# A graph network on one core: the opening written anew, and the turned tiles' move

## The reference

```
x = x + L0(relu(norm(x)))   # relu(mean over incoming edges @ W_l.T + b + x @ W_r.T)
x = x + L1(relu(norm(x)))   # two such convolutions with untransposed weights (L1A, L1B)
x = x + L2(relu(norm(x)))   # the means by src, residual, a layer norm with gamma and beta
x = x + L3(relu(norm(x)))   # two convolutions scaled by degrees, with self loops (L3A, L3B)
```

## Time and profile before

| | us |
|---|---|
| median of 3 runs (lowest to highest) | 646.88 (646.28 to 648.64) |
| the profiled execution | 647.0 |
| its span (first to last instruction) | 645.1 |
| PE busy | 626.6, 97% of the span |
| DVE, ACT, POOL busy | 401.5, 303.8, 85.2 |

### The profile page before, as it was taken

The page is one execution under the profiler, slowest core; times in us unless marked ns, Lnnn a source line. Parts: engine busy times, 40 slices in busy tenths (PEclk is TensorE's granted clock), DMA queues, the critical chain, the costliest instruction groups (busy, mean ns, idle before and its releaser), DMA issues.

```text
span 645.1 us, 11113 instructions
## 1 busy us (share of the span) xinstructions
PE 626.6 (97%) x3047; PEld 511.2 (79%) x3048; DVE 401.5 (62%) x875; ACT 303.8 (47%) x628; POOL 85.2 (13%) x135
## 2 busy tenths in 40 slices
PE   5989999999989999999999999999999999999997
PEld 4547767777868888888888888888888998899886
DVE  6998999977867434533434888754999730531222
ACT  4887886644423454431224342225478752565210
POOL 4442433200000000000000000000354070000000
PEclk9999999999999999999999999999999999999999
DMA  6300005457684422587550465431200000000102
GB/s 215 117 1 2 1 23 80 63 125 150 105 172 109 109 33 72 142 207 173 122 91 6 130 142 148 98 65 49 81 1 1 1 2 1 2 0 1 49 17 97
DMA packets 151843, 48.39 MB, mean 75 GB/s; under 512 B 133500, under 2 KB 137396, under 8 KB 151800
## 3 DMA queue, kind: packets, MB, share of 16 engines
q1 hardware_dynamic: 150520, 45.34, 30.8%
q10 hardware_dynamic: 1280, 2.56, 1.2%
HBM read 30.44 MB, written 17.44 MB: 74 GB/s over the span
## 4 chain that ended last, share of the span: by engine, by line
PE 86%; DVE 4%; DMA 3%; issue 2%; SPq 2%; ACT 1%; DVEq 1%; ACTq 0%
PE ps L1721 33%; PE ps L1814 23%; PE ps L1851 13%; PE ps L1877 8%; PE ps L1700 8%; DMA count_rows<-count_squares 2%; SPq L491 1%; DVE src_hot L1212 1%; DMA wstage<-in_L_gnn_W_l 1%; PE ps L1714 1%; DVE stats L1184 1%; DVE p_lo L1504 0%; ACT cstage L844 0%; DMA zT<-rows 0%; DVE own L1436 0%
## 5 line engine op out<-in xcount | busy, mean ns | idle before, releaser
L1814 PE MATMUL ps<-p_hi,cstage 128*128 128x512 f32 x400 | 156.0, 390 | 2.8 <-ACT cstage L844 2.8
L1814 PE MATMUL ps<-p_lo,cstage 128*128 128x512 f32 x400 | 155.7, 389 | 0.0
L1721 PE MATMUL ps<-w_hi,hT_hi 128*128 128x512 f32 x320 | 126.3, 395 | 0.6 <-issue 0.4
L1721 PE MATMUL ps<-w_hi,hT_lo 128*128 128x512 f32 x320 | 124.7, 390 | 0.0
L1721 PE MATMUL ps<-w_lo,hT_hi 128*128 128x512 f32 x320 | 124.6, 389 | 0.0
L1814 PEld LDWEIGHTS ps<-p_hi,cstage 128*128 128x128 f32 x400 | 75.1, 188 | 19.7 <-ACT cstage L844 2.9
L1814 PEld LDWEIGHTS ps<-p_lo,cstage 128*128 128x128 f32 x400 | 75.1, 188 | 15.5
L1212 DVE TENSOR_SCALAR src_hot<-iota,nodeT 128x640 bf16<-128x640 f16 x210 | 69.0, 384 | 5.8 <-PE ps L1700 3.7
L1700 PE MATMUL ps<-src_hot,dst_hot 128*128 128x320 bf16 x420 | 65.7, 305 | 5.8 <-DVE src_hot L1212 2.9
L1721 PEld LDWEIGHTS ps<-w_hi,hT_hi 128*128 128x128 f32 x320 | 60.1, 188 | 13.3 <-issue 0.9
L1721 PEld LDWEIGHTS ps<-w_hi,hT_lo 128*128 128x128 f32 x320 | 60.1, 188 | 12.7
(11 more groups left out here) (156 smaller groups left out, 941.3 us busy)
## 6 DMA issues: line engine op xcount, KB each, us to landing
rows<-squares SPq DMA_DIRECT2D x38, 256.0 KB, 2.5
zT<-rows SPq DMA_DIRECT2D x120, 64.0 KB, 2.5
count_rows<-count_squares SPq DMA_DIRECT2D x10, 320.0 KB, 2.2
countT<-count_rows SPq DMA_DIRECT2D x40, 80.0 KB, 3.2
x<-in_x ACTq DMA_DIRECT2D x1, 2304.0 KB
out_x<-x SPq DMA_DIRECT2D x9, 256.0 KB
wstage<-rows SPq DMA_DIRECT2D x32, 64.0 KB, 2.5
wstage<-in_L_gnn_W SPq DMA_DIRECT2D x2, 1024.0 KB, 5.7
```

Of the source, the lines that this page charges most:

```text
L1721: last = nc.tensor.matmul(ps[:, bank, :], a[:, r, k, :], w[:, slot, k, :], start=n == 0, stop=n == len(pairs) - 1)
L1814: last = nc.tensor.matmul(ps[:, AGG + r, :], cstage[:, part, k, :], p_[:, k, :], start=n == 1, stop=n == 2 * len(parts) * NT)
```

## The change

It has four parts. (1) The ranges of the windows are found without turning `reach`: each partition (an edge tile) says for all 20 windows whether it meets them (`begun`, `meets`), and an fp16 matmul of `meets` with a diagonal of tile numbers (`diag_ud`, made by POOL) puts the numbers of the meeting tiles on the window's partition; DVE then takes two maxima and derives `span` in fewer steps, and writes `tiles_of` of window 0 itself. (2) The keys are made by ACT (a copy with +1, a Sign, a copy, a scaled Sign) and POOL (a product and a sum) in fp16, and turned by fp16 matmuls with `ident16`. (3) Loads move: `src` is loaded by ACT's queue ahead of its table load; SP issues both halves of the first weight, the second weight and `x` one behind the other without waits; the first weight goes to `w_first` (in the space of `p_hi`). The turns and splits of the weights are dealt out differently around the first windows, POOL makes 2 of 20 windows of `tab` first and 18 after its keys, and `mv_now` with its copy is gone. (4) In L0, `first_tile` and DVE's `lo` of the next layer's tiles move from i = 5 and 6 to 6 and 7 (L1A and L1B keep theirs).

```diff
...
-    FIRST_W = (wstage, w_own)
+    FIRST_W = (w_first, w_own)
...
+    def load_edges(engine, k, dram, loaded):
+        engine.dma_start(e_int[:, k, 0, :], dram[0:P * P].rearrange("(t e) -> t e", e=P)).then_inc(loaded, 16)
+        engine.wait_ge(pads_set, 1)
+        engine.dma_start(e_int[0:FULL - P, k, 1, :],
+                         dram[P * P:FULL * P].rearrange("(t e) -> t e", e=P)).then_inc(loaded, 16)
+        if REST:
+            engine.dma_start(e_int[FULL - P:FULL - P + 1, k, 1, 0:REST],
+                             dram[FULL * P:E].rearrange("(t e) -> t e", t=1)).then_inc(loaded, 16)
...
+            load_edges(sp, 0, dst_dram, dst_loaded)
...
-            order = [("f", 0), ("f", 1), ("f", 2), ("v", rows[0]), ("v", rows[1])]
+            order = [("f", 0), ("f", 1), ("f", 2), ("x", None), ("v", rows[0]), ("v", rows[1])]
...
-                        sp.wait_ge(first_loaded[1], 16)
-                        sp.wait_ge(table_pe, 3)
-                        sp.wait_ge(table_step, steps_of_table)
...
+            nc.gpsimd.iota(tile_ud[:, 0, :], [[1, ETP]], base=1, channel_multiplier=0, **ramp).then_inc(ramps0, 1)
+            nc.gpsimd.iota(tile_ud[:, 1, :], [[-1, ETP]], base=ET, channel_multiplier=0, **ramp).then_inc(ramps0, 1)
+            nc.gpsimd.iota(block_lo[:, :], [[WIN, NW]], base=0, channel_multiplier=0, **ramp)
+            nc.gpsimd.iota(block_hi[:, :], [[WIN, NW]], base=WIN, channel_multiplier=0, **ramp)
+            nc.gpsimd.iota(fours[:, :], [[RING, ETP // RING]], base=ET, channel_multiplier=0, **ramp).then_inc(ramps0, 1)
             pool.wait_ge(ident0, 1)
             nc.gpsimd.affine_select(out=ident[:, :], in_=ident[:, :], compare_op=ALU.not_equal, fill=1.0,
-                                    base=0, pattern=[[-1, P]], channel_multiplier=1).then_inc(pool_consts, 1)
-            nc.gpsimd.iota(iota[:, :], [[1, NS]], base=0, channel_multiplier=0,
-                           allow_small_or_imprecise_dtypes=True).then_inc(pool_consts, 1)
-            for q, sign in ((0, 1), (1, -1)):
-                nc.gpsimd.iota(tab[:, :, q * WIN:(q + 1) * WIN], [[sign * WIN, NW], [sign, WIN]], base=sign,
-                               channel_multiplier=0, allow_small_or_imprecise_dtypes=True).then_inc(pool_consts, 1)
+                                    base=0, pattern=[[-1, P]], channel_multiplier=1).then_inc(ident0, 1)
+            pool.wait_ge(ramps0, 3)
+            nc.gpsimd.memset(fours[:, 0:1], -float(ETP))
+            for a, b in ((0, P), (P, ETP)):
+                nc.gpsimd.affine_select(out=diag_ud[:, :, a:b], in_=tile_ud[:, :, a:b], compare_op=ALU.is_equal, fill=0.0,
+                                        base=0, pattern=[[0, 2], [-1, b - a]], channel_multiplier=1).then_inc(diag_set, 1)
+            pool.wait_ge(ident0, 2)
+            nc.gpsimd.tensor_copy(ident16[:, :], ident[:, :]).then_inc(ident0, 1)
+            nc.gpsimd.iota(iota[:, :], [[1, NS]], base=0, channel_multiplier=0, **ramp).then_inc(tab_begun, 1)
+            def tab_of(a, b, done):
+                for q, way in ((0, 1), (1, -1)):
+                    nc.gpsimd.iota(tab[:, a:b, q * WIN:(q + 1) * WIN], [[way * WIN, b - a], [way, WIN]],
+                                   base=way * (1 + a * WIN), channel_multiplier=0, **ramp).then_inc(done, 1)
+            tab_of(0, 2, tab_begun)
...
+            pool.wait_ge(node_parts, 2)
+            nc.gpsimd.tensor_tensor(turned16[:, 0, :, :], e_f[:, 0, :, :], sign[:, :, :], ALU.mult).then_inc(keys_made, 1)
+            pool.wait_ge(node_parts, 4)
+            nc.gpsimd.tensor_tensor(turned16[:, 1, :, :], e_f[:, 1, :, :], shift[:, :, :], ALU.add).then_inc(keys_made, 1)
+            tab_of(2, NW, tab_full)
...
+            load_edges(act, 1, src_dram, src_loaded)
             act.wait_ge(dve_consts, 1)
             nc.scalar.activation(inner[:, 0, 3:4], eps[:, :], ACT.Sqrt)
-            for k, loaded in enumerate((dst_loaded, src_loaded)):
-                act.wait_ge(loaded, 16 * (2 + bool(REST)))
-                nc.scalar.copy(e_f[:, k, :, :], e_int[:, k, :, :]).then_inc(cast_done, 1)
-            act.wait_ge(first_loaded[1], 16)
-            act.wait_ge(x_pad_set, 1)
-            dma_rows(act, x_dram, x, x_loaded)
+            act.wait_ge(dst_loaded, 16 * (2 + bool(REST)))
+            nc.scalar.activation(e_f[:, 0, :, :], e_int[:, 0, :, :], ACT.Copy, bias=1.0).then_inc(node_parts, 1)
+            act.wait_ge(src_loaded, 16 * (2 + bool(REST)))
+            nc.scalar.activation(sign[:, :, :], e_int[:, 1, :, :], ACT.Sign, scale=-1.0, bias=middle[:, 0:1]
+                                 ).then_inc(node_parts, 1)
+            nc.scalar.copy(e_f[:, 1, :, :], e_int[:, 1, :, :]).then_inc(node_parts, 1)
+            act.wait_ge(node_parts, 2)
+            nc.scalar.activation(shift[:, :, :], sign[:, :, :], ACT.Copy, scale=NS / 2, bias=-NS / 2).then_inc(node_parts, 1)
...
-            split_first(0, range(0, 2))
-            act.wait_ge(table_step, steps_of_table)
-            act.wait_ge(pool_consts, 4)
+            act.wait_ge(table_step, FIRST_OF_TABLE)
+            act.wait_ge(tab_begun, 3)
...
             receivers(0, 0, visits_of(act, visited, 0, 0))
+            split_first(0, range(0, 2))
+            act.wait_ge(table_step, STEPS_OF_TABLE)
+            receivers(0, 1, visits_of(act, visited, 0, 1))
             split_first(0, range(2, KF))
-            receivers(0, 1, visits_of(act, visited, 0, 1))
             counts_of(0, 0)
+            act.wait_ge(tab_full, 2)
...
-                        if i == 5 + late // 2:
+                        if i == 5 + (s != L1A):
                             first_tile(0)
-                        if i == 6 + late // 2:
+                        if i == 6 + (s != L1A):
...
+            dve.wait_ge(ramps0, 3)
+            for g in range(2):
+                last = nc.vector.tensor_scalar(begun[:, g, :], block_lo[:, :], reach[:, g:g + 1], None, ALU.is_le)
+            step(last)
+            for g in range(2):
+                last = nc.vector.scalar_tensor_tensor(meets[:, g, :], block_hi[:, :], reach[:, 2 + g:3 + g],
+                                                      begun[:, g, :], ALU.is_gt, ALU.mult)
+            step(last)
             dve.wait_ge(table_pe, 1)
-            for k, tiles in enumerate((tile_up, tile_dn)):
-                last = nc.vector.scalar_tensor_tensor(marks[0:NW, k, :], ps[0:NW, TABLE, 0:ETP], block_lo[0:NW, 0:1],
-                                                      tiles[0:NW, :], ALU.is_ge, ALU.mult)
-            step(last)
-            for k in range(2):
-                last = nc.vector.scalar_tensor_tensor(marks[0:NW, k, :], ps[0:NW, TABLE, 256:256 + ETP],
-                                                      block_hi[0:NW, 0:1], marks[0:NW, k, :], ALU.is_lt, ALU.mult)
-            step(last)
-            step(nc.vector.tensor_reduce(ends[0:NW, :], marks[0:NW, :, :], AX_X, ALU.max))
-            step(nc.vector.tensor_scalar(low[0:NW, :], ends[0:NW, 1:2], 1.0, -1.0, ALU.max, ALU.mult))
-            step(nc.vector.scalar_tensor_tensor(length[0:NW, :], ends[0:NW, 0:1], -float(ET), low[0:NW, :],
-                                                ALU.add, ALU.subtract))
-            nc.vector.tensor_scalar(base[0:NW, :], low[0:NW, :], float(ET), None, ALU.add)
-            step(nc.vector.tensor_scalar(over[0:NW, :], fours[0:NW, :], length[0:NW, 0:1], None, ALU.is_lt))
+            step(nc.vector.tensor_reduce(ends[0:NW, :], ps[0:NW, TABLE, 0:2 * ETP].rearrange("p (k t) -> p k t", k=2),
+                                         AX_X, ALU.max))
+            dve.wait_ge(diag_set, 2)
+            nc.vector.tensor_scalar(base[0:NW, :], ends[0:NW, 1:2], -1.0, float(ET), ALU.mult, ALU.add)
+            step(nc.vector.tensor_scalar(over[0:NW, :], fours[0:NW, :], ends[0:NW, 0:1], ends[0:NW, 1:2],
+                                         ALU.subtract, ALU.is_lt))
             step(nc.vector.tensor_reduce(groups[0:NW, :], over[0:NW, :], AX_X, ALU.add))
-            step(nc.vector.scalar_tensor_tensor(span[0:NW, :], groups[0:NW, :], 256.0 * RING, base[0:NW, :],
-                                                ALU.mult, ALU.add))
-            dve.wait_ge(table_pe, 3)
-            step(nc.vector.tensor_copy(tiles_of[0:1, :], ps[0:1, TABLE, 0:NW]))
+            for to in (tiles_of[0:1, 0:1], span[0:NW, :]):
+                n = to.shape[0]
+                step(nc.vector.scalar_tensor_tensor(to, groups[0:n, :], 256.0 * RING, base[0:n, :], ALU.mult, ALU.add))
...
-                nc.vector.bn_aggr(mv_now[:, :], stats[:, :]).then_inc(aggr_done, 1)
-            def statistics_3(v, i):
-                dve.wait_ge(aggr_done, NT * v + i + 1)
-                nc.vector.tensor_scalar(mv[:, bass.ds(i, 1), :], mv_now[:, :].unsqueeze(1), 1.0, None,
-                                        ALU.mult).then_inc(mv_done, 1)
+                nc.vector.bn_aggr(mv[:, i, :], stats[:, :]).then_inc(mv_done, 1)
...
```

(62 more changed lines are left out.)

72 lines of the change are left out of this document (18 added, 54 removed).

## The result

The changed kernel takes 641.4 us (median of 5 runs, 640.94 to 642.1) where the kernel before took 646.88 beside it: ratio 0.9913, 95% interval 0.9897 to 0.993. Its profiled span is 639.1 us, 6.0 less.

What follows compares the result with a forecast made beforehand. PE is 97% busy; loss lies in the opening, the suppliers' pace up to 47.4 us and a 2.48 us wait in layer 0's sums. 647.0 - 2.8 - 0.5 - 2.5 = 641.2, median 641.1; range 639.0 to 643.6.

Steps and rivals of the forecast that it cites:

- the loads: Opening: `nodeT` no longer stands behind any load; the first weight's halves land at 6.0 and 7.5 us.
- the keys: Opening: ACT's instructions 4.0 to 5.5 us, POOL's product and sum 0.7 each, `nodeT` copied 7.0 to 7.45.
- the ranges: Opening, DVE's steps: `span` done at 7.05 us if never held; middle taken, first count 10.8, POOL's one-hot 12.5.
- the first tiles: Layer 0's sums: PE's stall of 2.48 us before tile 8 goes whole; gain 2.5, bounds 1.0 and 2.5.
- The clock step: First window: low clock cost POOL's five further rings 1.6 us; opening's gain 1.8 to 4 by its return, 2.8 taken.
- the sum: Whole kernel: 647.0 less 2.8 (opening), 0.5 (statistics) and 2.5 (layer 0's sums) gives 641.2 us, 641.1 for the median.
- The queue rival: Opening: SP's four loads share the engines instead of ending in order; first count about 19, 649.3 us; chance 0.04.
- Its 16.8: Opening, the queue rival: time in us when the first weight's first half lands, 12.2 after 3.9.
- The premise that `nodes_placed` at 10.83 opened everything: Opening of the kernel before: ACT's first `apart` comes 1.12 us after it, the first count 1.72 after that.
- the turns and splits dealt out anew: Around the first window: ACT's two splits and PE's eight transposes move behind it; price 0, at most 0.5 us.
- the upper bound: Opening: POOL's iotas hold DVE; first count 11.2, POOL's one-hot about 12.9, opening gives 1.8, time 642.2 us.
- Statistics: Ten copies of 0.17 us and their waits go, three up to 47.4 and one at 90; gain 0.5 in all.

Runs made afterwards that it cites:

- e5_tab_later: Changed kernel with the mask, POOL's `tab` for windows 2 to 19 moved behind its first one-hot, 6 to 19 behind its fourth: 640.58 us, ratio 0.989.
- e6_keys_after_ranges: e5_tab_later, and POOL also waits with the keys' product and sum until DVE has done `begun` and `meets`: 640.86 us, ratio 0.9898.
- e2: Kernel before with the mask and only the first tiles moved to i = 6 and 7 in layer 0: 645.44 us, ratio 0.9972.
- e4: Kernel before with the mask and the loads alone: x and `w_own` through SP's queue without waits: 647.24 us, ratio 1.0007.
- e3_clock_held: Kernel before with the mask and 30 more PE matmuls of zeros ahead of the first count: 648.87 us, ratio 1.0018.
- a0_again: Second, later run of the control, the changed kernel with only one mask more on each loop length: 640.59 us, ratio 0.9909.
- a0_control: First run of the control, the changed kernel with only one mask more on each loop length: 641.0 us, ratio 0.9912.
- e9: Changed kernel with the mask and layer 0's statistics as before (`mv_now`, a wait, DVE's copy, ten times): 641.9 us, ratio 0.9922.
- e1: Changed kernel with the mask and the first tiles back at i = 5 and 6 in layer 0: 643.51 us, ratio 0.995.
- e8: e5_tab_later with PE multiplying zeros in the opening (36 products, 7 more ahead of the matmul of `span`): 639.89 us, ratio 0.9894.
- b0: Kernel before with only one mask more on each loop length, no value changed: 649.36 us, ratio 1.0024.

## Why the prediction was right, and where its steps were off

The forecast was 641.1, the result 641.4. The mechanism was the predicted one in the loads, the keys, the ranges and the first tiles. The clock step had it wrong, the ranges were mis-sized, and the sum came so close partly by luck.

*Keys and loads: right, with one premise wrong.* Product and sum took 0.72 each (0.7 was taken), `nodeT` came at 7.46 for 7.0. ACT's casts began at 3.66, not 4.0. The profile has one load of tables (2.26, 1.28 long) and none at the Sign, which agrees with the Trainium skill (ScalarE: Activation LUTs, Table sets). The queue rival fell: the halves landed 3.7 and 4.7 us after issue, as before, and PE turned two chunks at 8.99, as soon as it had turned `span`. (Its 16.8 is 3.9 + 12.2 = 16.1; nothing hangs on it.) The premise that `nodes_placed` at 10.83 opened everything held for 0.4 us only: without it the count waits for `tiles_of` at 10.45. The loads alone and the loads put back show that this part is worth 0 to 1.1 us by itself and 1.0 to 1.8 behind the new ranges. No run tests by itself that the turns and splits dealt out anew cost nothing.

*Ranges: mis-sized.* `span` was to start between its two bounds, at 6.9 and 8.9 us, and started at 8.64; the first count was put at 10.8 and came at 11.43, past the 11.2 of the upper bound; POOL's one-hot was ready at 13.35, not 12.5, nor at the 12.9 of the upper bound. The step took the middle between "DVE is never held" and "DVE is held by the iotas". It was held by every long POOL instruction, the product and the sum too, which the upper bound had left out: 0.54, 0.41 and 0.53 us, the surplus of 0.91, 0.80 and 0.81 over the 0.37, 0.39 and 0.28 that the same instructions took when POOL stood. e5_tab_later and e6_keys_after_ranges show that by taking the holds away. The Trainium skill's rule (GPSIMD Engine Reference, Key points), that GpSimd contends with VectorE's instructions of both ports or two SBUF inputs, agrees with these runs but for `base`, and it was the better guide than my middle. POOL's lateness has a second part, read from the rows and not tested: in the new code VectorE reads its own loop bounds (`found = visits_of` in the diff) before it copies the other windows' `tiles_of`. The copy starts 0.72 after PE's product (8.84 + 0.22 = 9.06, 9.78), against 0.10 in the kernel before (10.18, 10.28), and POOL, which waits for it, has its one-hot 3.4 behind its end at 9.95. The hold by the iota matters 0.6 us at the first count and less in the whole time: e5_tab_later's median is 0 to 0.4 under the two runs of the control, which the intervals don't separate.

*The clock: this step failed.* It put 1.6 us of the first window down to the granted clock of 0.50 and let the gain hang on whether that came again. The number came true: in the changed kernel POOL's five further rings took 9.80 (13.35 to 23.15) instead of 11.63, with the clock at 1.00. But the row is not what decides. Two kernels with the old opening (e2, e4) had a full clock in that row and were no faster there, their sixth one-hots starting at 25.65 and 25.34 against 25.25 in the base with the same mask, whose clock stood at 0.50. What they share is the pace: in every kernel but e3_clock_held count matmuls near the start took about 474 ns, for 1 to 4 us. In the kernel before and its masked base this began at about 14.6, after some matmuls at 299, in the others with the first count. Five profiles have the changed opening as it is and differ in how long the slow pace lasted: until about 12.5 in the changed kernel, 12.6 in a0_again, 13.8 in a0_control, 14.3 in e9 and 14.8 in e1. Their sixth one-hots start at 22.32, 22.43, 22.71, 22.87 and 22.89. By my estimate from these, each microsecond of slow pace costs a quarter of one there. In e5, e6 and e8, which begin earlier, it lasted until about 14.5, and of a head start of 0.4 to 0.7 over the controls at most 0.4 was left at the sixth one-hot (22.30, 22.50, 22.29). What sets its length stays open; e3 and e8 show that zeros ahead of the counting don't turn it into time.

*Statistics: size not shown.* 0.5 was taken; the medians differ by 0.9 to 1.3, within intervals that overlap, and the profiles do not tell the copies from the spread of one and the same code. So it is open what made the counting 1.01 shorter. From the first count to the sixth one-hot it is 0.39 (11.28 and 10.89), where the copies play no part and the slow pace was shorter; the other 0.62 come behind it. It made up for the late first count: together they gave 3.25, where the sum had 2.8 + 0.5.

*First tiles: right.* PE's wait of 2.48 went whole and the sums became 2.98 shorter, down to PE's own time; nothing later took its place, the next layer's first product began 6.14 earlier (189.41 for 195.55) for 5.8 forecast. The moved tiles are worth 2.5 in the changed kernel and 3.4 over the masked kernel before, where the clock fell after the wait.

*The sum.* In the profiles 3.25 up to the first product and 2.98 in the sums, less 0.1 in the middle: 6.1 for 5.8. The medians give 5.5.

## What to carry to other kernels

When a change removes the chain that the profile calls critical, look for the second one and time it too: here it stood 0.4 us behind, and the loads were worth 0 to 1.1 us until the second chain had been shortened too. Where VectorE and GpSimd work side by side on a chain of short steps, add to each VectorE step the rest of whatever GpSimd instruction may be running, products and sums as well as iotas, and place GpSimd's long instructions where VectorE's chain doesn't pass. A wait of TensorE in a full stage can cost more than its length, for its clock may fall behind it, so price it from the stage's length with and without it. And before a difference between two profiles is given a cause, look where it begins: a part of e9_copy_back's was there before the first instruction that could cause it.

## What the runs showed of the hardware

- GpSimd may be held the other way round as well. In the masked kernel before, one of its one-hots of 128x128, 0.6 to 1.6 us elsewhere, took 2.69 and ended at 34.22, beside a series of VectorE instructions without a gap from 31.88 to 34.5. No run tests it, and 3.03 at the same place in e3_clock_held is the only other such row:

```profile
31.53 2.69 POOL L607 TENSOR_SCALAR dst_hot<-tab_now,key_now 128x128 bf16<-128x128 f16 x1 [1.76 <-PE ps L1700]
```

- A count matmul (320 columns) lasts 474 ns at the slow pace and 299 at the full one, and the granted clock in the profile showed the slow pace in three kernels (before, b0, e8) and stood at 1.00 in ten others that had it too.
- A register instruction more for each loop length read made layer 0's first product 0.8 to 1.1 us later with the old opening (the whole kernel 1.5, ratio 1.0024) and cost nothing that was measured with the new one.
